# Selecting matrices waited for at their use, and zero columns that make whole pieces of the rank products

## The reference

```python
x = x + L0(x, ...)   # a long convolution with a kernel built from exponentials, masked by length
x = x + L1(x, ids1)  # einsum('bsi,boi->bso', x, weight[ids1]): each sequence picks one of 16 matrices
x = x + L2(x, ids2)  # the same with other weights
x = x + L3(x, ids3)  # gated MLP, F = 2752, with low-rank additions picked by sequence

def lora_add(base, inp, A, B):                     # rank 16, SCALE = 0.5
    t = einsum('bri,bni->bnr', A[ids3], inp)
    return base + einsum('bor,bnr->bno', B[ids3], t) * SCALE
gate = lora_add(x @ W_gate.T, x, A_gate, B_gate)
up   = lora_add(x @ W_up.T,   x, A_up,   B_up)
act  = silu(gate) * up
down = lora_add(act @ W_down.T, act, A_down, B_down)
```

## Time and profile before

| | us |
|---|---|
| median of 3 runs | 2102.03 |
| lowest, highest | 2098.35, 2105.87 |
| the profiled execution | 2097.59 |
| its span, first to last instruction | 2095.9 |
| TensorE busy | 2018.3 |
| VectorE busy | 1786.5 |
| ScalarE busy | 1007.3 |
| GpSimd busy | 141.4 |

### The profile page before, as it was taken

The page is one execution under the profiler, slowest core; times in us unless marked ns, Lnnn a source line. Parts: engine busy times, 40 slices in busy tenths (PEclk is TensorE's granted clock), DMA queues, the critical chain, the costliest instruction groups (busy, mean ns, idle before and its releaser), DMA issues.

```text
span 2095.9 us, 34321 instructions
## 1 busy us (share of the span) xinstructions
PE 2018.3 (96%) x10124; PEld 1714.4 (82%) x10124; DVE 1786.5 (85%) x2248; ACT 1007.3 (48%) x1259; POOL 141.4 (7%) x239
## 2 busy tenths in 40 slices
PE   3999999999997999999999999999999999999999
PEld 3898888878886878888888888887888888888887
DVE  8796999989997888888888779978888888877777
ACT  2122888878885543434334443354334343334332
POOL 3100000000002222210000030000000000000000
PEclk9999999999998999999999999999999999999999
DMA  7997999989999467663333996554343434468565
GB/s 253 339 328 285 356 360 354 354 329 349 350 356 346 121 188 207 202 182 108 115 113 110 339 304 227 196 171 123 113 115 113 124 110 112 117 213 308 200 210 186
DMA packets 263681, 471.07 MB, mean 225 GB/s; under 512 B 115462, under 2 KB 119750, under 8 KB 243910
## 3 DMA queue, kind: packets, MB, share of 16 engines
q1 hardware_dynamic: 246498, 427.58, 60.0%
q0 software_dynamic: 14944, 42.50, 6.7%
q10 hardware_dynamic: 2180, 0.26, 0.1%
HBM read 430.10 MB, written 63.73 MB: 236 GB/s over the span
## 4 chain that ended last, share of the span: by engine, by line
PE 83%; DVE 9%; DMA 3%; ACT 2%; issue 2%; POOL 1%; DVEq 0%; ACTq 0%; SPq 0%
PE ps L2367 19%; PE ps L2368 19%; PE ps L2369 19%; PE ps L2289 5%; PE ps L2290 5%; PE ps L2291 5%; PE ps L2261 5%; PE ps L2465 3%; DMA W<-in_w 2%; PE ps L2298 1%; PE ps L2502 1%; PE ps L2503 1%; DVE part L1610 1%; DMA traw<-kept_acts 1%; DMA wraw<-in_wd 1%
## 5 line engine op out<-in xcount | busy, mean ns | idle before, releaser
L2367 PE MATMUL ps<-rows,oph 128*128 128x512 f32 x1196 | 471.6, 394 | 1.2 <-ACT tmp L1017 0.6
L2368 PE MATMUL ps<-rows,oph 128*128 128x512 f32 x1196 | 466.6, 390 | 0.0
L2369 PE MATMUL ps<-rows,opl 128*128 128x512 f32 x1196 | 465.9, 390 | 0.0
L1610 DVE TENSOR_TENSOR part<-W,part 128x2048 fp32r<-128x2048 f32 x152 | 344.3, 2288 | 14.6 <-ACT part L952 13.6
L952 ACT ACTIVATE part<-W 128x2048 fp32r<-128x2048 f32 x152 | 291.0, 1917 | 89.1 <-DMA W<-in_w 63.7
L1705 DVE TENSOR_TENSOR tmp<-ps,tmp 128x512 f32<-128x512 f32 (+2 forms) x344 | 243.0, 707 | 69.8 <-PE ps L2465 54.4
L2369 PEld LDWEIGHTS ps<-rows,opl 128*128 128x128 f32 x1196 | 224.8, 188 | 48.7
L2367 PEld LDWEIGHTS ps<-rows,oph 128*128 128x128 f32 x1196 | 225.3, 188 | 45.0 <-DVE opl L1702 2.0
L2368 PEld LDWEIGHTS ps<-rows,oph 128*128 128x128 f32 x1196 | 225.2, 188 | 42.1
L2367 PE MATMUL ps<-th,wdh 128*128 128x512 f32 (+1 forms) x656 | 249.5, 380 | 2.4 <-DVE tl L1702 1.6
L2368 PE MATMUL ps<-tl,wdh 128*128 128x512 f32 (+1 forms) x656 | 248.5, 379 | 0.0
(11 more groups left out here) (252 smaller groups left out, 2960.7 us busy)
## 6 DMA issues: line engine op xcount, KB each, us to landing
W<-in_w SPq DMA_DIRECT2D x152, 1024.0 KB, 7.1
raw<-in_wgu SPq DMA_DIRECT2D x168, 256.0 KB, 3.0
traw<-kept_acts SPq DMA_DIRECT2D x78, 512.0 KB, 4.9
wraw<-in_wd SPq DMA_DIRECT2D x70, 512.0 KB
toep<-kpad SPq DMA_DIRECT2D x31, 1024.0 KB, 8.5
kept_acts<-tmp SPq DMA_DIRECT2D x84, 256.0 KB, 2.4
lraw<-picked_b SPq DMA_DIRECT2D x176, 96.0 KB, 2.1
lraw<-picked_b SPq DMA_DIRECT2D x176, 64.0 KB, 1.9
```

The source lines that it names most:

```text
L1610: V.tensor_tensor(out=wl[c][:], in0=W[:, c], in1=wh[c][:].bitcast(F32), op=ALU.subtract).then_inc(w_lo, 1)
L2367: mm(to, lhsT=wh, rhs=mh, start=start, stop=False)
L2368: mm(to, lhsT=wh, rhs=ml, start=False, stop=False)
L2369: return mm(to, lhsT=wl, rhs=mh, start=False, stop=stop)
```

## The change

Nothing that is computed changes. The parts:

- The matmul queue waits for `sel_set` only in the first `place_ranks`, no longer ahead of the MLP.
- Each row of `tm` gets 64 columns more, between the first and the second outer span (`TERMS_AT`). GpSimd clears them for the one row that bank C reads, before each stage, as a second step of `clear`; the counts of `cleared` double. With them the two outer pieces of bank C are whole halves (`WHOLE_SPANS`), and the middle span is one piece: three products of 256 columns in place of five.
- The second `place_ranks` stands after six of the twelve B22 products, not after all.
- ScalarE's copies for `tt` come in another order, with a semaphore `tt_set` of their own for the last; `tm` copies of the first stage stand ahead of the copy of T3, and in the second stage the copy of A11 stands ahead of them.
- VectorE cuts both `tt` before the `lt` of the half unit. In the units the `lt` subtraction of the next unit stands ahead of `v_lo1`, in unit 1 ahead of the last `lo` too.

```diff
--- before.py
+++ after.py
@@ -91,8 +91,9 @@
 PLACE_BANK, PLACE_REST = 6, 4
 
 SPANS = ((0, 3 * H), (5 * H, 8 * H), (2 * H, 6 * H))
-TERMS_AT = (0, 3 * H, 6 * H)
-TERMS = 10 * H
+TERMS_AT = (0, 4 * H, 7 * H)
+TERMS = 11 * H
+WHOLE_SPANS = ((0, 4 * H), (4 * H, 8 * H), (2 * H, 6 * H))
 RANK_ROWS = (((0, 0, 48), (48, 0, 48), (96, 0, 32)),
              ((0, 80, 48), (48, 80, 48), (96, 96, 32)),
              ((0, 48, 32), (32, 48, 32), (64, 32, 64)))
@@ -100,7 +101,7 @@
 CHOSEN = (((0, 0, 48), (48, 64, 48), (96, 0, 32)),
           ((0, 16, 48), (48, 80, 48), (96, 32, 32)),
           ((0, 48, 16), (16, 0, 16), (32, 112, 16), (48, 64, 16), (64, 32, 32), (96, 0, 32)))
-assert GC == 4 * H and 2 * GC == TILE and 3 * TERMS_AT[1] + H == TERMS
+assert GC == 4 * H and 2 * GC == TILE and TERMS_AT[2] + GC == TERMS
 
 
 
@@ -409,6 +410,7 @@
         bop_lo = sem("bop_lo")
         tm_part = sem("tm_part")
         tm_hi = sem("tm_hi")
+        tt_set = sem("tt_set")
         tt_lo = sem("tt_lo")
         sel_set = sem("sel_set")
         placed_done = sem("placed_done")
@@ -572,7 +574,7 @@
                     part = slice(k * SEQ, (k + 1) * SEQ)
                     sp.dma_start(xs[:, part], X[:, part]).then_inc(x_saved[k], 16)
                 next_last(0)
-                sp.wait_ge(cleared, 1)
+                sp.wait_ge(cleared, 2)
                 load_down_ranks(0, 0)
 
             def load_last():
@@ -597,7 +599,7 @@
                 next_last(st)
                 sp.wait_ge(panel_done, sides(st, 0))
                 load_ranks(st, 0)
-                sp.wait_ge(cleared, st + 1)
+                sp.wait_ge(cleared, 2 * st + 2)
                 load_down_ranks(st, 0)
 
             def store_acts(st, u):
@@ -804,6 +806,8 @@
             def clear(st):
 
                 pool.memset(ahl[HALF:P].rearrange("p j h w -> p (j h w)").bitcast(F32), 0.0).then_inc(cleared, 1)
+                pool.wait_ge(cleared, 2 * st + 1)
+                pool.memset(tm[:, 1, 1, SPANS[0][1]:WHOLE_SPANS[0][1]].bitcast(F32), 0.0).then_inc(cleared, 1)
 
             def store(st, ready, j, half):
 
@@ -885,6 +889,7 @@
                 for to, at, n in pieces:
                     last = pool.tensor_copy(sel[k][:, to:to + n], ident[:, at:at + n])
             last.then_inc(sel_set, 1)
+            pool.wait_ge(sel_set, 1)
 
 
             pool.wait_ge(t3_raw, 1)
@@ -1074,13 +1079,15 @@
 
                 act.wait_ge(tm_part, st * 2 + j + 1)
                 copy(thl[j][0:HALF, 0], sraw[0:HALF, 2 + j])
-                copy(thl[j][0:HALF, 1], sraw[HALF:P, 2 + j])
                 copy(thl[j][HALF:P, 1], sraw[HALF:P, 2 + j]).then_inc(tm_hi, 1)
+                copy(thl[j][0:HALF, 1], sraw[HALF:P, 2 + j]).then_inc(tt_set, 1)
 
             def ranks_placed(st, j):
 
                 act.wait_ge(placed_done, st * 2 + j + 1)
-                copy(tm[:, j, :, 0:2 * TERMS_AT[1]], ps[:, PLACE_BANK:PLACE_BANK + 2, 0:2 * TERMS_AT[1]])
+                ends = 3 * H
+                copy(tm[:, j, :, 0:2 * TERMS_AT[1]].rearrange("p c (k w) -> p c k w", k=2)[:, :, :, 0:ends],
+                     ps[:, PLACE_BANK:PLACE_BANK + 2, 0:2 * ends].rearrange("p c (k w) -> p c k w", k=2))
                 copy(tm[:, j, :, TERMS_AT[2]:TERMS], bank(PLACE_REST).rearrange("p (c w) -> p c w", c=2)
                      ).then_inc(tm_set, 1)
 
@@ -1149,8 +1156,6 @@
 
             def half_unit(st):
 
-                if st:
-                    hi(st, 1, A11)
                 for i in (S2, A12, S1):
                     hi(st, 1, i)
                 act.wait_ge(unit_step, at_step(st, 0, 4))
@@ -1320,10 +1325,11 @@
             act.wait_ge(x_saved[0], 16)
             for st in range(NST):
                 if st:
-                    act.wait_ge(cleared, st + 1)
+                    act.wait_ge(cleared, 2 * st + 2)
                     ranks_projected(st, 0)
                     ranks_projected(st, 1)
                     ranks_hi(st, 0)
+                    hi(st, 1, A11)
                     ranks_placed(st, 0)
                     ranks_placed(st, 1)
                 else:
@@ -1335,8 +1341,8 @@
                     hi(st, 1, A11)
                     ranks_projected(st, 1)
                     ranks_placed(st, 0)
+                    ranks_placed(st, 1)
                     operand_hi(T3, rraw[LO[T3]][:])
-                    ranks_placed(st, 1)
                 half_unit(st)
                 unit(st, 1)
                 with act.Fori(2, FT - 1) as one:
@@ -1926,12 +1932,12 @@
                 v_silu1(st, 1)
                 lo(st, 2, 5)
                 v_act1(st, 1)
+                ranks_lo(st, 2)
+                v_lo1(st, 1)
                 lo(st, 2, 6)
-                v_lo1(st, 1)
 
             def unit(st, u):
 
-                ranks_lo(st, u)
                 down_ranks_lo(st, u - 1)
                 add_weights(st, u + 1)
                 lo(st, u + 1, 0)
@@ -1954,6 +1960,7 @@
                 lo(st, u + 1, 6)
                 v_silu1(st, u)
                 v_act1(st, u)
+                ranks_lo(st, u + 1)
                 v_lo1(st, u)
 
             def cut_side_lo(st, n):
@@ -2186,7 +2192,7 @@
             dve.wait_ge(mask_set, 4)
             for st in range(NST):
                 if st:
-                    dve.wait_ge(cleared, st + 1)
+                    dve.wait_ge(cleared, 2 * st + 2)
                 ranks_part(st, 0)
                 if st == 0:
                     dve.wait_ge(t_raw, 1)
@@ -2197,13 +2203,11 @@
                     dve.wait_ge(t4_raw, 1)
                 ranks_part(st, 1)
                 ranks_cut(st, 0)
+                ranks_cut(st, 1)
                 ranks_lo(st, 0)
                 if st == 0:
                     dve.wait_ge(x_saved[1], 16)
-                    lo(st, 1, A11)
-                ranks_cut(st, 1)
-                if st:
-                    lo(st, 1, A11)
+                lo(st, 1, A11)
                 half_unit(st)
                 with dve.Fori(2, FT - 1) as one:
                     unit(st, one)
@@ -2368,9 +2372,9 @@
                 mm(to, lhsT=wh, rhs=ml, start=False, stop=False)
                 return mm(to, lhsT=wl, rhs=mh, start=False, stop=stop)
 
-            def row_blocks(to, hi, lo, i, start=False, stop=False):
-
-                for k in range(KH):
+            def row_blocks(to, hi, lo, i, start=False, stop=False, some=range(KH)):
+
+                for k in some:
                     cols = slice(k * P, (k + 1) * P)
                     last = three(to, hi[:, cols], lo[:, cols], rows[HI[i]][:, k], rows[LO[i]][:, k],
                                  start and k == 0, stop and k == KH - 1)
@@ -2437,15 +2441,19 @@
                 last.then_inc(ap_done, 4)
                 row_blocks(bank(BANK_D), kop[:, 0], kop[:, 1], T1)
                 place_ranks(0, 0)
-                row_blocks(bank(BANK_D), kop[:, 2], kop[:, 3], B22)
+                row_blocks(bank(BANK_D), kop[:, 2], kop[:, 3], B22, some=range(2))
                 place_ranks(0, 1)
+                row_blocks(bank(BANK_D), kop[:, 2], kop[:, 3], B22, some=range(2, KH))
 
             def place_ranks(st, j):
 
+                if st == 0 and j == 0:
+                    pe.wait_ge(sel_set, 1)
+                pe.wait_ge(tt_set, st * 2 + j + 1)
                 pe.wait_ge(tt_lo, st * 2 + j + 1)
                 if j:
                     pe.wait_ge(tm_set, st * 2 + 1)
-                ends, rest = TERMS_AT[1], TERMS_AT[2]
+                ends, rest = 3 * H, 6 * H
                 for c in range(2):
                     src = thl[j][:, c]
                     mm(ps[:, PLACE_BANK + c, 0:ends], lhsT=sel[0], rhs=src[:, SPANS[0][0]:SPANS[0][1]], start=True, stop=True)
@@ -2456,14 +2464,10 @@
 
             def add_ranks(to, c, j, stop, start=False):
 
-                pieces = [(k, a, b) for k, (a, b) in enumerate(SPANS)]
-                if start:
-                    low, high = SPANS[0][1], SPANS[1][0]
-                    pieces[2:] = [(2, SPANS[2][0], low), (2, low, high), (2, high, SPANS[2][1])]
-                for n, (k, a, b) in enumerate(pieces):
+                for k, (a, b) in enumerate(WHOLE_SPANS if start else SPANS):
                     at = TERMS_AT[k] - SPANS[k][0]
                     last = mm(ps[:, to, a:b], lhsT=lt[:, k, j, c], rhs=tm[:, j, c, at + a:at + b],
-                              start=start and n == 0, stop=stop and n == len(pieces) - 1)
+                              start=start and k == 0, stop=stop and k == 2)
                 return last
 
             def half_unit(st):
@@ -2480,13 +2484,15 @@
                     blocks(bank(BANK_D), K0, T1, start=True)
                     blocks(bank(BANK_D), K0, B11)
                     place_ranks(st, 0)
-                    blocks(bank(BANK_D), K1, B22)
+                    row_blocks(bank(BANK_D), oph[:, K1], opl[:, K1], B22, some=range(2))
                     place_ranks(st, 1)
+                    row_blocks(bank(BANK_D), oph[:, K1], opl[:, K1], B22, some=range(2, KH))
```

(2 more changed lines are left out.)

## The result

| | before | after |
|---|---|---|
| median | 2100.19 (4 runs) | 2072.11 (4 runs) |
| lowest, highest | 2095.94, 2105.87 | 2070.92, 2075.76 |
| the profiled execution | 2097.59 | 2071.13 |
| its span | 2095.9 | 2069.5 |

The ratio is 0.9868, 95% interval 0.9839 to 0.9896: faster by 28.1 us by the medians, where 22.5 was forecast. The changed kernel was measured twice more beside the experiments: 0.9887 (0.9868 to 0.9906) and 0.9864 (0.9847 to 0.9880), 24.1 and 28.1 us.

A forecast was written before the change was run, and what follows sets the result against it. The matmul engine, 96% busy, was taken as the bound, held at the start by a 14.2 us wait for data needed only later. Terms 13.5 + 0.5 + 3.5 + 5.0 = 22.5 us off 2102.03 gave 2079.5 us; range 2070 to 2090.

The forecast's parts named there:

- the C ranks: Each of 42 units: three products for five gain 0.12 us a unit, 5.0 us in all, bounds 2.5 and 8.4.
- The moved wait: Start of the MLP: matmuls no longer wait for the selecting matrices and follow VectorE's blocks; 13.5 us gained.
- upper bound of 14.4: Start of the MLP: gain in us if rank products run at full clock, paced by VectorE; lower end 10.9.
- The ranks of the first stage: Placings up to unit 2, first stage: loss of 0.7 and gain of 1.2; 0.5 us taken, bounds -0.5 and 1.5.
- ScalarE is still busy: First stage, second masked tile: ScalarE must first copy `tt`, `lt` and `oph`, put at 0.7 us of delay.
- what is late next is the activation's low part: Unit 2: 1.2 us of the `lt` wait goes; the activation's low part comes at nearly the same time as `lt`.
- The ranks of the second stage: Second stage, placings and unit 2: unit 1 1.8 us earlier, `lt` wait 1.2 us less; 3.5 us, bounds 1.5 and 5.0.
- itself long at 0.48 us: Product behind the C ranks, 0.48 us where 0.40 is usual: may lose its extra 0.08 us.
- take over in the start: Rival, chance 0.11: VectorE sets the pace in the start and slips by half the gain, 7 us; 2086.5 us.
- Not dearer: Rival, chance 0.07: narrow products were not dearer, so the C ranks lose 2 us instead of gaining 5; 2086.5 us.
- Doesn't do what it says: Rival, chance 0.06: the wait returns at the first placing because `tt` is late; 5 to 6 us left, 2096.5.
- The slower case: Rival, chance 0.04: late `lt` delays the activation's low part, 0.7 us in each unit, 29.4 us lost; 2108.9 us.

The follow-up runs named there:

- e1: The kernel before with only the wait for the selecting matrices moved into the first placing: 2083.15 us, ratio 0.9935.
- e4: The kernel before with only VectorE's `lt` subtractions moved ahead of the activation's low part: 2096.79 us, ratio 1.0002.
- a1: The changed kernel with VectorE's `adt` subtraction directly behind the activation's low part: 2068.56 us, ratio to the kernel before 0.9873.
- e3: The kernel before with only the placing edits (second placing after six B22 products, copy order, both `tt` cut in a row): 2097.03 us, ratio 0.9991.
- a3: The changed kernel with one VectorE subtraction of 2.28 us in the start done twice: 2072.36 us, beside 2069.13 for the changed kernel.
- e2: The kernel before with only the zero columns and three whole products for bank C: 2090.65 us, ratio 0.9968.
- a2: The changed kernel with bank C's middle span in two products of 128 columns, four products for three: 2076.90 us, ratio to the kernel before 0.9898.
- a4_both: The changed kernel with `adt` cut early and, in the second stage, ScalarE's A11 copy behind the first `tm` copy: 2070.59 us, ratio to before 0.9874.
- a0_again: The changed kernel unchanged, measured a second time as the measure for the runs beside it: 2073.26 us.
- a1_second: Repeat of the changed kernel with `adt` cut directly behind the activation's low part: 2072.26 us, beside 2069.13 for the changed kernel.
- a0_second: The changed kernel unchanged, measured a third time as the measure for the runs beside it: 2069.13 us.

## Why the prediction was right, and where it was off

The change gained 24 to 28 us by the medians, for 22.5, and its 2072.1 us lie near the low end of the range of 2070 to 2090. In the profiled pair the change itself is worth 23.2 us. That this is so near 22.5 is in part luck: the C ranks brought 3.5 us more than was counted, and 1.6 us at the lower clock and 0.9 us of longer waits, for which the sum had no term, took most of it back.

**The moved wait: right, 14.1 for 13.5.** Products from 654.02, VectorE's blocks as the pace, `kop` 7.9 us after the first low part, no gap of 9.72 us on VectorE: each as foretold. The clock stayed up, so the gain came near the upper bound of 14.4. Where the clock does fall after the small waits, as in e1, it is 13.24. The choice between the ends was a choice about this, and no trace says which of the two an execution will show: four of nine traces with this start have the fall.

**The ranks of the first stage: right in sum (0.3 for 0.5), wrong in its parts.** "ScalarE is still busy" was to cost 0.7 us up to the placing; instead 1.06 us were gained there, since ScalarE came in time for the second placing. The 1.2 us that the earlier `lt` was to bring in unit 2 came to 0.20. And VectorE took back 0.98 in unit 1, where `lt`, `adt` and `ahl` follow each other without a break: a wait for `ahl` appeared:

```profile
696.16 0.36 PE L2508 MATMUL ps<-ahl,adt 128*128 128x256 f32 x1 [0.96 <-DVE ahl L1708]
```

The failed step is "what is late next is the activation's low part". It is the low part of the down ranks, one `opl` subtraction of 0.69 us further back in VectorE's queue:

```profile
718.90 1.92 DVE L1708 TENSOR_TENSOR lt<-lraw,lt 32x1024 fp32r<-32x1024 f32 x2
720.85 0.69 DVE L1708 TENSOR_TENSOR ahl<-tmp,ahl 128x512 fp32r<-128x512 f32 x1
721.46 0.68 DVE L1708 TENSOR_TENSOR opl<-sraw,oph 128x512 fp32r<-128x512 f32 x1
722.06 0.42 DVE L1708 TENSOR_TENSOR adt<-adraw,adt 128x256 fp32r<-128x256 f32 x1
```

`project_down` needs both, and I had looked at one of its two operands. e4 and a1 show it.

**The ranks of the second stage: 2.8 for 3.5, within the bounds.** The `tm` wait of 0.7 us that was foretold is there, at 0.61:

```profile
1387.57 0.25 PE L2459 MATMUL ps<-tt,sel_ends 128*128 128x192 f32 x1
...
1390.41 0.33 PE L2459 MATMUL ps<-tt,sel_ends 128*128 128x192 f32 x1 [0.61 <-ACT tm L1022]
...
1392.56 1.53 PE L2469 MATMUL ps<-tm,lt 128*128 128x192 f32 x12
```

The twelve rank products run in one piece at full clock, and unit 1 starts 1.83 us earlier, for "1.8 us". The 0.9 us that the higher clock was to give on top are not there: e1, which still has both waits and no slow stretch, reaches unit 1 only 0.2 us sooner than the kernel before and gives it back at its down product, where VectorE's `ahl` then holds the engine for 1.14 us in place of 0.50. The clock cost nothing, since VectorE set the pace. The forecast had missed this wait. With the slow products ahead of it, it is what the next 1.44 us are: with both `tt` cut first it is gone, in e3 too, and the stretch from unit 1 to there takes 8.67 us for 10.11 before and 10.31 in e1. For `lt` 1.2 us had been counted. The stretch up to the down product of unit 2 lost 0.44 in this pair, with 1.13 us of wait for `adt`; the later traces put it between a loss of 0.1 and a gain of 0.15, and e4 gains 0.30. The failed step is the same as in the first stage.

**The C ranks: the mechanism right, the size too small, 9.0 for 5.0.** This is the term with the largest error, and the one that makes the sum too small. Each unit gains 0.21 us, not 0.12. The 0.11 us of the C products themselves lie at the top of the 0.06 to 0.12 foretold. What I mis-sized is the delay behind them: I saw that the product behind is "itself long at 0.48 us" and counted almost nothing for it, when the trace before already gave the whole. There these twelve products took 2.83 us, the twelve behind the three rank products of bank F 2.76 (753.37 to 756.13), and the twelve with only wide products ahead of them 2.72 (756.13 to 758.85):

```profile
756.13 0.39 PE L2367 MATMUL ps<-rows,oph 128*128 128x512 f32 x1
...
758.85 0.39 PE L2367 MATMUL ps<-rows,oph 128*128 128x512 f32 x1
```

Now the twelve behind the C ranks take 2.72 as well, so 0.11 goes away here too. Even my bound of 0.20 a unit was passed. With 8.5 for the 40 C ranks that lie outside the ranks' stretches and the other terms as measured the sum is 14.1 + 0.3 + 2.8 + 8.5 = 25.7 us; the three comparisons gave 28.1, 24.1 and 28.1.

The Trainium skill, "TensorE: Matmul & The Clock Gate", section "Back-to-back issue gap", puts an isolated product at columns / 2.4 + 2.5 ns with a floor near 25 ns, which I had set against this edit. By it C's ranks would take an estimated 0.28 us as five, 0.33 as four and 0.33 as three. The traces have 0.48, 0.42 and 0.37, and differ from it most where there are most products; here the measurements decide. The same section says itself that the formula counts too little for narrow products in a stream in which each has its weight load, which the forecast left out. The traces agree: every product here has a weight load (10040 of each), and the five take 0.20 us more than the formula gives.

**The rivals.** VectorE did not take over in the start: it still had 0.78 us of idle time ahead of the second mask. But a3 shows that the margin is nil on the path through ScalarE, so a kernel in which VectorE has 2.3 us more to do there loses 2.3 us. "Not dearer" fell with e2 and a2. "Doesn't do what it says" fell: no wait stands ahead of the first placing. The slower case needed `lt` to be late in every unit; in the loop units no `lt` or `ahl` wait appears at all, and the 0.7 us of `lt` waits are the two of unit 2.

**Side by side.** The four ratios alone give 13.6 + 6.7 + 1.9 - 0.4 = 21.8 us, the whole 24 to 28. Each carries an uncertainty of about 2.5 us, so the difference says nothing of an interplay; the traces, which agree to 0.15 us a stretch up to the down product of unit 1 in each stage, show none beyond the clock.

## What to carry to other kernels

A wait that stands ahead of work which doesn't need it is worth its whole length only as far as the engines behind can follow: read their idle time up to the next common point, and not on the direct path alone, but on each path that a third engine carries. Products of 64 to 192 columns cost nearly what those of 256 do (0.10 us each for 0.12, as means of the five and the three), in themselves and again in the products behind them, so compare stretches of equal work with and without narrow products in front, and count the difference fully. When a low part is moved forward to end a wait, list all operands of the waiting instruction: the next late one may stand just behind, and then almost nothing is gained.

## What the runs showed of the hardware

**The clock falls after some clusters of short waits, in some executions.** In the start of the MLP TensorE has waits of 0.69, 0.68 and 0.36 us within 4 us, in the same code, in e1 and in all traces of the changed kernel and its variants (the first is 1.17 us in a3 and 0.96 in a4_both). In e1, a0_again, a1_second and a4_both the granted clock then fell to 0.50 for some 3 us; in the changed kernel's own profile, a0_second, a1_adt_first, a2 and a3 it did not. It costs 0.85 us there (8.76 us from the first low part to `kop` in a0_again, 7.91 after). Ahead of the down product of unit 2 in the second stage stands a wait of 1.13 us. In the changed kernel:

```profile
1426.00:1428.00 2.00, 1.35 (x9) 1.36 (x10) 2.00 (x5) 0.00 (x0) 0.00 (x0) 0.84 0.62 181
1428.00:1430.00 2.00, 2.00 (x6) 1.61 (x6) 1.97 (x4) 0.63 (x1) 0.00 (x0) 0.50 0.38 122
```

and in a0_again, the same program, where that wait stands at 1427.68:

```profile
1426.00:1428.00 2.00, 0.88 (x5) 0.68 (x6) 2.00 (x4) 0.00 (x0) 0.00 (x0) 1.00 0.70 235
1428.00:1430.00 2.00, 2.00 (x14) 1.78 (x13) 1.97 (x4) 0.53 (x1) 0.00 (x0) 1.00 0.64 181
```

From there to the down product of the next unit it is 1449.78 - 1426.65 = 23.13 us in the first and 21.56 in the second: 1.57 us. This is the last row of the table above; a0_second shows it as well. In a2 and a3, with the same wait, it did not fall. It isn't peculiar to the changed kernel either. Behind the long wait for `lt` or `adt` in unit 2 of the first stage the clock fell in e2, e3 and e4 (waits of 1.70, 1.73 and 1.13 us), and the stretch to the next down product took 1.6 us more, 23.37 us for 21.77 in e4; in the kernel before and in e1, with 1.74 and 1.70 us, it stayed up. In e4, where the down product of unit 2 stands at 738.53:

```profile
738.00:740.00 2.00, 1.47 (x9) 1.48 (x10) 2.00 (x5) 0.00 (x0) 1.12 (x2) 0.81 0.84 270
740.00:742.00 2.00, 2.00 (x7) 1.52 (x6) 1.97 (x4) 0.63 (x1) 0.00 (x0) 0.50 0.89 245
```

So a single pair of traces can differ by 1.6 us in either direction at such a place. Why one execution falls and the other doesn't stays open; with the wait at 0.5 us, in a1_adt_first, a1_second and a4_both, no fall was seen there, but three traces don't prove that none comes.

**Up to 256 columns, the number of products weighs more than their columns.** 640 columns in five products cost 0.48 us, 768 in four 0.42, 768 in three 0.37, and the twelve wide products behind them 2.83, 2.80 and 2.72. That a few more products slow those behind them by as much as they take themselves was not expected. Products of 512 columns take 0.23 us each, so this doesn't carry on to the widest ones. Whether the delay comes from the weight loads that stand close together was not tried.
